# Turning the second chunk's queries and the first chunk's residual by VectorE blocks and transfers through DRAM

## What is computed

```python
x = x + attn(layernorm(x))      # 16 heads of 32
#   q, k, v = split(xn @ W_qkv + b_qkv)
#   gate = sigmoid(xn @ W_gate + b_gate); gate /= mean(gate) + eps
#   q = relu(q * gate)**2 + eps;  k = relu(k * gate)**2 + eps
#   kv_s += k (x) v;  k_s += k;   out = (q . kv_s) / (q . k_s + eps)
#   attn = out @ W_proj + b_proj
x = x + ffn(layernorm(x))       # P = x@U1; H = gelu(P@V1 + b1); Q = H@U2; Q@V2 + b2
```

## Time and profile before

| | |
|---|---|
| median of 3 runs | 1697.15 us (1697.0 to 1698.67) |
| the profiled execution | 1697.67 us |
| its span | 1695.9 us |
| PE busy | 1665.1 us, 98% |
| DVE busy | 1400.3 us, 83% |
| POOL busy | 900.2 us, 53% |
| ACT busy | 630.5 us, 37% |
| HBM traffic | 67 GB/s over the span |

### The profile page before, as it was taken

One profiled execution on the slowest core, in us unless ns is written; L12 is line 12 of the kernel. 1 busy time (PEld: TensorE's weight loads), 2 busy tenths in 40 slices (PEclk: granted clock), 3 DMA queues, 4 the chain that ended last, 5 costly groups with the idle time before them and its releaser, 6 DMA issues.

```text
span 1695.9 us, 39553 instructions
## 1 busy us (share of the span) xinstructions
PE 1665.1 (98%) x16221; PEld 1401.9 (83%) x16221; DVE 1400.3 (83%) x2223; ACT 630.5 (37%) x1178; POOL 900.2 (53%) x1026
## 2 busy tenths in 40 slices
PE   6899999999999999999999999999999999999998
PEld 4688888888888888888888888888888888888876
DVE  6888888888888888888888888888888888888875
ACT  4233333333333333433433333333333333333332
POOL 3355555555555555555555555555555555555540
PEclk9999999999999999999999999999999999999999
DMA  8323323333322333342333233343223323322210
GB/s 231 88 58 70 59 75 46 72 75 57 72 72 45 74 70 60 73 71 47 74 72 59 73 62 56 74 69 61 74 49 69 75 57 70 74 45 73 58 45 26
DMA packets 206324, 115.67 MB, mean 68 GB/s; under 512 B 151144, under 2 KB 161792, under 8 KB 206144
## 3 DMA queue, kind: packets, MB, share of 16 engines
q1 hardware_dynamic: 205280, 111.57, 31.4%
q10 hardware_dynamic: 864, 1.57, 0.5%
HBM read 79.38 MB, written 33.72 MB: 67 GB/s over the span
## 4 chain that ended last, share of the span: by engine, by line
PE 93%; DVE 3%; DMA 1%; issue 1%; SPq 1%; ACT 0%; POOL 0%; DVEq 0%; POOLq 0%
PE ps_a L849 11%; PE ps_a L850 10%; PE ps_a L851 10%; PE scores L849 8%; PE scores L851 8%; PE scores L850 8%; PE ps_h L849 4%; PE ps_h L850 4%; PE ps_h L851 4%; PE scores L980 4%; PE scores L1008 4%; PE ps_q L849 3%; PE ps_q L850 3%; PE ps_q L851 3%; PE scores L856 3%; PE ps_a L1026 2%
## 5 line engine op out<-in xcount | busy, mean ns | idle before, releaser
L447 POOL TENSOR_TENSOR h_lo<-h_full,h_hi 128x512 fp32r<-128x512 f32 x244 | 336.4, 1389 | 220.4 <-DVE h_hi L665 219.0
L849 PE MATMUL ps_a<-wx_hi,zt_hi 128*128 128x512 f32 x768 | 315.7, 411 | 6.3 <-DVE key_sums L787 4.2
L850 PE MATMUL ps_a<-wx_lo,zt_hi 128*128 128x512 f32 x768 | 305.1, 397 | 0.0
L851 PE MATMUL ps_a<-wx_hi,zt_lo 128*128 128x512 f32 x768 | 305.0, 397 | 0.0
L530 ACT ACTIVATE h_full<-ps_h,cols 128x256 f32<-128x256 f32 x512 | 204.5, 476 | 144.1 <-PE ps_h L851 137.6
L849 PEld LDWEIGHTS ps_a<-wx_hi,zt_hi 128*128 128x128 f32 x768 | 145.3, 189 | 43.2 <-DVE zt_lo L620 7.1
L665 DVE CAST h_hi<-h_full 128x512 fp32r<-128x512 f32 x256 | 163.3, 648 | 17.8 <-ACT h_full L530 13.7
L851 PEld LDWEIGHTS ps_a<-wx_hi,zt_lo 128*128 128x128 f32 x768 | 145.1, 189 | 35.6
L850 PEld LDWEIGHTS ps_a<-wx_lo,zt_hi 128*128 128x128 f32 x768 | 145.3, 189 | 28.7 <-issue 0.5
L541 ACT ACTIVATE query_t<-scores 128x512 f32<-128x512 f32 x64 | 38.3, 599 | 345.9 <-PE scores L856 345.9
L467 POOL TENSOR_TENSOR key_lo<-keys,key_hi 128x512 fp32r<-128x512 f32 x64 | 86.9, 1358 | 121.1 <-ACT key_hi L561 121.1
(11 more groups left out here) (156 smaller groups left out, 4230.7 us busy)
## 6 DMA issues: line engine op xcount, KB each, us to landing
xs<-L_attn_x SPq DMA_DIRECT2D x64, 256.0 KB, 4.1
key_blocks<-zs SPq DMA_DIRECT2D x64, 256.0 KB, 2.0
key_t<-key_blocks SPq DMA_DIRECT2D x256, 64.0 KB
out<-x1s SPq DMA_DIRECT2D x64, 256.0 KB, 2.1
xt<-x_turned SPq DMA_DIRECT2D x63, 256.0 KB, 4.2
key_sums<-carry_rows SPq DMA_DIRECT2D x60, 256.0 KB, 3.7
rows<-turned_rows SPq DMA_DIRECT2D x63, 64.0 KB, 4.5
x1s<-L_attn_W_gate SPq DMA_DIRECT2D x4, 256.0 KB, 4.2
```

Of the source, the lines that this page charges most:

```text
L447: E.tensor_tensor(h_lo[:, i % SLOTS, :], h_full[:, i % SLOTS, :], h_hi[:, i % SLOTS, :].bitcast(F32), ALU.subtract).then_inc(s["h_lo_ready ...
L849: E.matmul(ps, wh, mh, start=start and i == 0, stop=False)
L850: E.matmul(ps, wh, ml, start=False, stop=False)
L851: mm = E.matmul(ps, wl, mh, start=False, stop=stop and i == last)
```

## The change

In even steps TensorE makes no transposes.

- The queries of a chunk with half 1: VectorE transposes them in blocks of 32x32 at the end of the odd step, behind L805, into `probs[:, 1]`. SP, behind the carry row's store, stores this to `qry_dram`, waits for the landing and loads it back into `query_t` in four DMAs, one for each 32 partitions. The scores of the even step wait for all four. TensorE's transposes and ScalarE's copy remain in odd steps only.
- The residual z1 of a chunk with half 0: VectorE transposes `zs` in blocks in the even step, behind L691 and ahead of L696, into `probs[:, 0]`. SP stores that to `res_dram` behind the carry row's load and ahead of `load_x`, waits for the landing at the start of its next step, and loads it into `zs` in four DMAs. ScalarE makes `x1t_hi` of it behind the last GELU of the even step, VectorE `x1t_lo` between L822 and L830.
- `zs` holds the residual during the even step, so the keys' block transpose goes to `gate` in all steps. L794, which writes `gate`, waits for that store in place of L830. L741 waits in even steps for the residual's store to have landed.

```diff
@@ -58,6 +58,10 @@
+    def pair(self, per=1):
+        return per * ((4 * self.p + self.off) // 2 + 1)
     def done(self, per=1, i=1):
...
@@ -338,6 +344,14 @@
         load_tiles((range(FIRST + 6, FIRST + 9), range(FIRST + 9, len(tiles)))[b])
+    d = Chunk(p, b - 2)
+    if d.exists and d.half == 0:
+        sp.wait_ge(s["res_out"], d.pair(16))
+        for j in range(HPG):
+            sp.dma_start(zs[j * HEAD:(j + 1) * HEAD, :].rearrange("d (f a t) -> d f a t", f=KT, t=HEAD),
+                         res_dram.rearrange("(a d) (f j t) -> j d f a t", d=HEAD, f=KT, t=HEAD)[j])\
+                .then_inc(res_in[j], 16)
     if b % 2:
@@ -348,7 +362,7 @@
             wait(sp, key_t_in[j], Chunk(p, b - 1).done(16, 16))
-        sp.dma_start(blocks_dram, zs[:, :]).then_inc(s["blocks_out"], 16)
+        sp.dma_start(blocks_dram, gate[:, :]).then_inc(s["blocks_out"], 16)
     means_out(Chunk(p, b + 2))
@@ -365,6 +379,17 @@
             .then_inc(carry_out[c.slot], 16)
+    if c.exists and c.half:
+        sp.wait_ge(s["qry_ready"], c.pair())
+        for j in range(HPG):
+            wait(sp, query_t_in[j], c.pair(16) - 16)
+        sp.dma_start(qry_dram, probs[:, 1, :]).then_inc(s["qry_out"], 16)
+        sp.wait_ge(s["qry_out"], c.pair(16))
+        for j in range(HPG):
+            sp.dma_start(query_t[j * HEAD:(j + 1) * HEAD, :, :].rearrange("d f (a t) -> d f a t", t=HEAD),
+                         qry_dram.rearrange("(a d) (f j t) -> j d f a t", d=HEAD, f=KT, t=HEAD)[j])\
+                .then_inc(query_t_in[j], 16)
     after = Chunk(p, b + 1)
@@ -372,6 +397,13 @@
             .then_inc(s["carry_in"], 16)
+    before = Chunk(p, b - 1)
+    if before.exists and before.half == 0:
+        sp.wait_ge(s["res_ready"], before.pair())
+        for j in range(HPG):
+            wait(sp, res_in[j], before.pair(16) - 16)
+        sp.dma_start(res_dram, probs[:, 0, :]).then_inc(s["res_out"], 16)
     load_x(Chunk(p, b + 3))
@@ -536,8 +568,8 @@
     pairs = range(4) if b % 2 else range(4, 8)
-    if c.exists:
-        act.wait_ge(s["tq_done"], c.done())
+    if c.exists and c.half == 0:
+        act.wait_ge(s["tq_done"], c.pair())
         E.activation(query_t[:, :, :].rearrange(flat), ps_t[:, :], ACT.Copy)\
@@ -546,8 +578,8 @@
         tile_heads(early_tiles)
-    if d.exists:
-        act.wait_ge(s["tx_done"], d.done())
+    if d.exists and d.half:
+        act.wait_ge(s["tx_done"], d.pair())
         E.activation(x1t_hi[:, :, d.half * P:(d.half + 1) * P],
@@ -571,6 +603,12 @@
         gelu(ffn, pairs[3])
+    if d.exists and d.half == 0:
+        for j in range(HPG):
+            act.wait_ge(res_in[j], d.pair(16))
+        E.activation(x1t_hi[:, :, 0:P], zs[:, :].rearrange("p (k n) -> p k n", k=KT), ACT.Copy)\
+            .then_inc(s["x1t_hi_ready"], 1)
+    if ffn.exists:
         if b % 2 == 0:
@@ -675,13 +713,23 @@
     finishing = is_last(p)
-    def x1t_tail():
+    def x1t_tail(turned):
...
             part = slice(d.half * P, (d.half + 1) * P)
-            E.tensor_tensor(x1t_lo[:, :, part], ps_t[:, :].rearrange("p (k n) -> p k n", k=KT),
+            E.tensor_tensor(x1t_lo[:, :, part], turned[:, :].rearrange("p (k n) -> p k n", k=KT),
                             x1t_hi[:, :, part].bitcast(F32), ALU.subtract).then_inc(s["x1t_ready"], 1)
+    def x1t_from_bank():
+        if d.half:
+            x1t_tail(ps_t)
+    def turn_residual():
+        if d.exists and d.half == 0:
+            dve.wait_ge(s["z1_ready"], d.done())
+            E.transpose(probs[:, 0, :], zs[:, :]).then_inc(s["res_ready"], 1)
@@ -691,6 +739,7 @@
             .then_inc(s["gate_evac"], 1)
+        turn_residual()
@@ -702,9 +751,10 @@
         squared_relu(n, s["key_done"], s["key_steps"], ps_b, KEY, keys[:, n.half, :],
-                     x1t_tail)
+                     x1t_from_bank)
     else:
-        x1t_tail()
+        turn_residual()
+        x1t_from_bank()
     if b % 2:
@@ -716,10 +766,12 @@
     if n.exists:
-        if c.exists:
-            dve.wait_ge(s["tq_done"], c.done())
+        if not c.exists:
+            add_rows(1)
+        elif c.half:
+            dve.wait_ge(s["qry_ready"], c.pair())
         else:
-            add_rows(1)
+            dve.wait_ge(s["tq_done"], c.pair())
         squared_relu(n, s["query_done"], s["query_steps"], ps_a, QUERY, queries[:, :])
@@ -728,16 +780,12 @@
         dve.wait_ge(s["key_ready"], n.done())
-        if d.exists:
-            dve.wait_ge(s["tx_done"], d.done())
-        elif c.exists:
-            dve.wait_ge(s["blocks_out"], c.done(16, 16))
-        else:
-            dve.wait_ge(s["tz_done"], 1)
-        E.transpose(zs[:, :], keys[:, n.half, :]).then_inc(s["blocks_ready"], 1)
+        E.transpose(gate[:, :], keys[:, n.half, :]).then_inc(s["blocks_ready"], 1)
     if c.exists:
...
         blocks = HPG * KT
+        if d.exists and d.half == 0:
+            dve.wait_ge(s["res_out"], d.pair(16))
         E.tensor_tensor(probs[:, :, :].rearrange("p j (k t) -> p (j k) t", k=KT),
@@ -791,6 +839,7 @@
         dve.wait_ge(s["query_steps"], n.done(3, 3))
+        dve.wait_ge(s["blocks_out"], n.done(16, 16))
         E.scalar_tensor_tensor(out=gate[:, :], in0=queries[:, :], scalar=EPS, in1=key_sums[:, :],
@@ -805,6 +854,10 @@
                                op0=ALU.add, op1=ALU.mult).then_inc(den_steps, 1)
+        if n.half:
+            dve.wait_ge(den_steps, n.done(6, 6))
+            E.transpose(probs[:, 1, :], queries[:, :]).then_inc(s["qry_ready"], 1)
     if c.exists:
@@ -820,13 +873,16 @@
         E.bn_aggr(moments1[:, :], stats1[:, :]).then_inc(s["x1_steps"], 1)
+    if d.half == 0:
+        x1t_tail(zs)
+    if c.exists:
         dve.wait_ge(s["x1_small"], c.done(2, 2))
-        if d.exists:
-            dve.wait_ge(s["tx_done"], d.done())
+        if d.exists and d.half == 0:
+            dve.wait_ge(s["x1t_ready"], d.done())
+        if d.exists and d.half:
+            dve.wait_ge(s["tx_done"], d.pair())
         elif not c.p and not c.off:
             dve.wait_ge(s["tz_done"], 1)
-        if n.exists:
-            dve.wait_ge(s["blocks_out"], n.done(16, 16))
         E.tensor_scalar(zs[:, :], x1s[:, c.slot, :], moments1[:, 0:1], small1[:, 1:2],
@@ -931,11 +987,11 @@
             pe.wait_ge(s["stage_lo"], 3 * KT)
-    if d.exists:
+    if d.exists and d.half:
         pe.wait_ge(s["z1_ready"], d.done())
-        if c.exists:
-            pe.wait_ge(s["query_t_ready"], c.done())
+        if c.exists and c.half == 0:
+            pe.wait_ge(s["query_t_ready"], c.pair())
         else:
@@ -969,8 +1025,12 @@
             pe.wait_ge(key_t_in[j], c.done(16, 16))
-        pe.wait_ge(s["query_t_ready"], c.done())
-        if d.exists:
+        if c.half:
+            for j in range(HPG):
+                pe.wait_ge(query_t_in[j], c.pair(16))
+        else:
+            pe.wait_ge(s["query_t_ready"], c.pair())
+        if d.exists and d.half:
             pe.wait_ge(s["x1t_ready"], d.done())
...
```

More of the change, by code:

```diff
@@ L108, in block_kernel @@
 def block_kernel(nc, x, ln_g, ln_b, w_qkv, b_qkv, w_gate, b_gate, w_proj, b_proj,
-                 u1, v1, b1, u2, v2, b2, x_turned, out, carry_dram, rows_dram, blocks_dram):
+                 u1, v1, b1, u2, v2, b2, x_turned, out, carry_dram, rows_dram, blocks_dram, res_dram, qry_dram):
     ctx = ExitStack()
@@ L207, in block_kernel @@
             query_done query_steps value_done value_ready
-            sums_done den_steps blocks_ready blocks_out tq_done query_t_ready
+            sums_done den_steps qry_ready qry_out blocks_ready blocks_out res_ready res_out tq_done query_t_ready
             scores_done probs_ready state_done state_ready ot_done ot_hi_ready ot_ready
@@ L215, in block_kernel @@
         xt_in = [sem(f"xt_in{i}") for i in range(4)]
+        res_in = [sem(f"res_in{j}") for j in range(HPG)]
+        query_t_in = [sem(f"query_t_in{j}") for j in range(HPG)]
         key_t_in = [sem(f"key_t_in{j}") for j in range(HPG)]
@@ L1069 @@
     carry_dram = nc.dram_tensor("carry_rows", (BATCHES, DM), _mybir.dt.float32, kind="Internal").ap()
+    qry_dram = nc.dram_tensor("query_blocks", (P, DM), _mybir.dt.float32, kind="Internal").ap()
     blocks_dram = nc.dram_tensor("key_blocks", (P, DM), _mybir.dt.float32, kind="Internal").ap()
+    res_dram = nc.dram_tensor("residual_blocks", (P, DM), _mybir.dt.float32, kind="Internal").ap()
     rows_dram = nc.dram_tensor("turned_rows", (BATCHES, P), _mybir.dt.float32, kind="Internal").ap()
-    block_kernel(nc, *args, out, carry_dram, rows_dram, blocks_dram)
+    block_kernel(nc, *args, out, carry_dram, rows_dram, blocks_dram, res_dram, qry_dram)
     r = _run(nc, [arrays], core_ids=[0])
```

## The result

The changed kernel takes 1797.12 us, the median of 4 runs (1789.87 to 1801.39), against 1697.08 us of the kernel before beside it (1694.59 to 1698.67). The ratio is 1.0587, 95% interval [1.055, 1.0623]: slower by 5.9%, where 1.5% faster was forecast.

The account below looks back on a forecast made before the run. TensorE, busy 98% of the span, was taken as the bound: 1697.67 - 27.0 + 0.9 = 1671.6 us profiled, 1671.1 as median. Chance 0.64 for 1668 to 1680, 0.84 for 1667 to 1700.

Parts of the forecast that it names:

- The step that failed: SP, even step: keys' blocks stored some 2 us later than 840.97, harmless because wanted only 20 us on.
- the loads behave like key_t in the steady state: Rival: query loads take 8.8 us, land 3.5 us after the scores want them; 1780 us, chance 0.11.
- the bound of 4.95 us for the loads: Program start: key_t's four loads, first issue 47.17, scores 52.12, so four query loads take at most 4.95 us.
- TensorE's saving: Even step, GATE to first h product: eight transposes cost 0.87 us; 31 steps give 27.0 us.
- The table load and the residual's transpose: Even step: ScalarE's table load runs ahead, L696 comes at 834.4, and VectorE's 0.70 us transpose is hidden.
- the masked copy: VectorE's L741, even step: starts about 840.1, ends 842.4, against 842.75 where TensorE wants it; 0.35 left.
- VectorE is now about 0.75 us earlier: Even step: x1t_lo leaving its place between the key steps, plus 0.15 at L696, puts VectorE about 0.75 us ahead.
- VectorE becomes the bound: Rival: table load stays behind L691, L741 ends at 843.7; 34 us lost, 1705 us, chance 0.05.
- The queries' way: Through DRAM: store landed at 833.1, four loads 4.6 us, queries there at 837.7 against the scores at 838.38.
- the second case of the prediction: Rival: transfers arrive a little late, about 0.6 us of TensorE's time a pair, 19 us; 1690 us, chance 0.20.
- The residual's way: Even step: store lands at 838.3, upper end 840.4, against L741 at 840.1; likely no cost, at worst 1.0 late.
- Start and end: First pairs not costed, good for 1 us either way; step 64 makes the end 0.9 us later.

Follow-up runs that it names:

- own: Changed kernel with the product of queries and key sums written to the free query_t instead of gate; 1704.72 us.
- best: ownpool with the residual's blocks turned into the values' buffer instead of probs; 1679.88 us.
- ends: best with the queries of chunks 1, 3 and 63 turned by TensorE as in the kernel before; 1666.31 us.
- nox: Changed kernel with both block transposes made but nothing stored, loaded back or awaited from DMA; 1695.72 us.
- ownpool: own with GpSimd's addition of the projection bias moved behind the centering in even steps; 1697.7 us.
- nomeans: Changed kernel without the 128 single-element row-means store and its waits in even steps from step 6 on; 1712.91 us.

## Why the prediction was wrong, point by point

**The step that failed** is the sentence "SP is held until about 843, so the keys' blocks go out some 2 us later than 840.97; they are wanted in the next step's scores, 20 us on". Its first half is right, a little small: the store goes out 14.6 to 17.6 us into the even step (median 16.0) instead of 12.5. The second half counts one reader of the store's landing and forgets the other. The change itself had moved a wait for it to VectorE's L794, in the same step, some 5 us behind the new issue; I didn't ask, for this wait, what is queued behind it. With a landing of 2.0 us it would still have been harmless. The second missing piece is that this median was read from steps in which the store had landed before the single-element stores came; the 8.4 us of step 0, in the same trace, wasn't looked at. What the runs showed in place of "wanted 20 us on": 115.7 us of waits at L843 in 24 instances. `own` has none of them, and is 92 us faster. The rival "the loads behave like key_t in the steady state" had the right culprit (the 128 single elements), at the wrong transfer: it was weighed for the queries' loads, not for the keys' store. Its 1780 us is near the result by chance. One of its premises was misread too: at the start the single elements had not "long landed". They were issued at 39.21 and took 8.5 us, so they landed at 47.7, behind key_t's first issue at 47.17; the bound of 4.95 us for the loads holds all the same.

**TensorE's saving** was right (36 x 0.234 is 8.42 and not 8.41, which changes nothing): GATE, KEY and QUERY take 8.40 us without a gap.

```profile
872.00 0.39 PE L905 MATMUL ps_a<-wx_hi,zt_hi 128*128 128x512 f32 x1
...
880.40 0.28 PE L905 MATMUL ps_h<-pt_hi,v_hi 128*128 128x256 f32 x1
```

`best` and `ends` show the whole 0.87 us of each even step arriving at the end of the program once three obstacles are out of the way.

**The table load and the residual's transpose** went as forecast, the masked copy didn't:

```profile
875.76 0.74 DVE L739 SCALAR_TENSOR_TENSOR gate<-ps_a,small,bias 128x512 f32<-128x512 f32 x1
876.42 0.70 DVE L732 STREAM_TRANSPOSE probs<-zs 128x512 f32<-128x512 f32 x1
877.30 0.15 DVE L745 TENSOR_SCALAR gate_scale<-gate_sum 128x1 f32<-128x1 f32 x1 [0.17 <-ACT gate L577]
...
878.70 1.67 DVE L694 SCALAR_TENSOR_TENSOR keys<-keys,gate_scale,gate 128x512 f32<-128x512 f32 x1
```

The wait at L745 (L696 before) fell from 1.69 us to 0.17: the load runs ahead. But "VectorE is now about 0.75 us earlier" was reckoned with the old duration of L694 (L656 before, 1.0 us). I had asked what GpSimd does to x1t_lo at its new place, and not to the steps that stay. Until 402 us GpSimd's addition comes 0.73 us later, at 7.18 us into the even step, since the transpose's 0.74 us goes into GpSimd's order as well; L694 is held for 1.9 us. After that VectorE has caught up with the slower TensorE: the addition is back at 6.5 us into the step, L694 begins at 6.7 instead of 7.3, and it is held for 1.63 to 1.67. Either way it ends 0.55 us behind the addition, at 9.0 or 8.4 us into the step, where the old end was 8.3. Its price is 0.5 us of wait and 0.7 of the step (24.06 in `nox` against 23.38 in `best`), some 20 us in all; that is near the case of "VectorE becomes the bound", from another cause.

**The queries' way**: the loads were sized well, the store was not. It landed in 2.0 to 5.4 us (median 4.2), against the 3.1 forecast and 3.6 as the upper end. The four loads took 4.3 to 4.7 us from the first issue to the last landing. In the step above they are issued at

```profile
877.32 2.63 SPq L390 DMA_DIRECT2D query_t<-query_blocks  x4
...
881.91 1.17 PE L1040 MATMUL scores<-query_t,key_t 32*128 32x128 f32 x32
```

and the scores start 4.59 us later, against the 4.6 of the text. The scores waited for them in 16 of 32 steps, 19.3 us in all: 10.3 in the first and the last of these steps, and 1.6 at most in each of the others, which is the second case of the prediction. In `own`, where SP is not held as long and the store lands in 2.0 to 4.1 us, the scores wait only in the first and the last. The bound from the start of the program was the right row to take.

**The residual's way**: its upper end was true. In steps 4 to 62 the store lands in 3.3 to 4.7 us, where the upper end had 4.1. L789 waited for the store in 24 steps (33.0 us), as in `ownpool` in 28.

**Start and end** were left at 1 us. The start costs 6.6 us in L843's first wait and 5.5 behind it, the end 3.4. The transfer's 8 us lie open wherever TensorE has little else, which also holds for the first pairs. At the end the scores come 8.0 us behind the last division, as reckoned (8.1); the other 2.5 us lie behind them and are not followed up here.

## What to carry to other kernels

When a store is moved later, list every semaphore wait on its landing, the ones that the change itself moves above all, and give the buffer that it reads to nobody who is in a hurry; one other buffer was worth 92 us here. A short landing time in a profile belongs to its neighbours in the queue, and a median hides the one that was long (8.4 us in step 0): look at what is issued within 2 us behind it as well as ahead. And a delay put into one engine's order has to be followed into the orders that hang on it; check VectorE's two-operand instructions against GpSimd's at the new times.

## What the runs showed of the hardware

- A 256 KB store whose packets had all begun 3.2 us after its issue completed only 11.1 us after it, together with a store of 128 single elements issued 1.95 us behind it; without the latter such stores landed in 2.2 to 4.7 us (29 steps of `nomeans`). At 1.76 us of distance both outcomes occur.
- The 128 single elements, 0.5 KB, take 7.6 to 9.9 us to land in the even steps of the changed kernel, more than 256 KB do.
- VectorE's second key step and GpSimd's addition, each with two operands of 128x512 in SBUF, are not both slowed a little when they overlap: one takes its usual time (0.75 or 1.29 us), and the other is held. If it is VectorE's, it ends 0.55 us behind GpSimd's; if it is GpSimd's, it takes 1.84 us. Where VectorE's starts 0.05 to 0.07 us ahead in the trace, either can be the one held.
